# One core, gated cross-attention and quantised FFN: VectorE takes a slot's row maxima before the slot's other work

## The reference

```
x = x + tanh(g_xattn) * attention(layernorm(x), ctx)   # 16 heads of 16, rotary q and k, |i - j| <= 50, softmax, Wo
x = x + tanh(g_ffn)   * ffn(layernorm(x))              # 4-bit weights, 16-bit quantised activations, 256 -> 768 -> 256
```

## Time and profile before

| | us |
|---|---|
| median of 3 runs | 1548.13 (1544.25 to 1549.3) |
| the profiled execution's own time | 1547.24 |
| its span, first to last instruction | 1545.5 |
| TensorE busy in the span | 1308.7 (85%) |
| VectorE busy | 1264.0 (82%) |
| ScalarE busy | 827.3 (54%) |
| GpSimd busy | 675.6 (44%) |

### The profile page before, as it was taken

One profiled execution on the slowest core, in us unless ns is written; L12 is line 12 of the kernel. 1 busy time (PEld: TensorE's weight loads), 2 busy tenths in 40 slices (PEclk: granted clock), 3 DMA queues, 4 the chain that ended last, 5 costly groups with the idle time before them and its releaser, 6 DMA issues. The chain is left out here.

```text
span 1545.5 us, 31329 instructions
## 1 busy us (share of the span) xinstructions
PE 1308.7 (85%) x8992; PEld 847.5 (55%) x8992; DVE 1264.0 (82%) x3572; ACT 827.3 (54%) x1328; POOL 675.6 (44%) x1407
## 2 busy tenths in 40 slices
PE   2469999979898998979799876998999788874998
PEld 1446777656575665657567542443433333333887
DVE  5678998969787887969698734998999899995886
ACT  2225665646455463646456544665777466672332
POOL 0247777758676675757577640000000154541000
PEclk7679999999999998989899987999999989996999
DMA  3257566564736454546365411223454343434675
GB/s 103 70 118 161 131 149 153 137 148 99 168 97 146 113 132 110 137 109 146 97 160 141 101 35 41 102 102 130 175 195 174 122 163 129 157 132 136 228 231 176
DMA packets 132351, 206.89 MB, mean 134 GB/s; under 512 B 11160, under 2 KB 97051, under 8 KB 126107
## 3 DMA queue, kind: packets, MB, share of 16 engines
q1 hardware_dynamic: 132250, 205.86, 47.8%
HBM read 125.60 MB, written 79.69 MB: 133 GB/s over the span
## 5 line engine op out<-in xcount | busy, mean ns | idle before, releaser
L727 DVE CUSTOM_DVE_ANT_0 psum<-psum,band 128x178 f32<-128x178 f32 x1024 | 320.0, 372 | 62.8 <-PE psum L855 38.1
L607 ACT ACTIVATE probs<-psum 128x356 f32<-128x356 f32 x512 | 209.3, 461 | 295.5 <-PE psum L872 295.5
L1030 PE MATMUL psum<-xnT,w_upT 128*128 (+1 forms) x1152 | 269.7, 394 | 48.0 <-ACT u_int L1418 30.0
L538 POOL TENSOR_SCALAR_AFFINE_SELECT probs<-probs 128x154 f32<-128x154 f32 (+1 forms) x512 | 214.1, 427 | 218.5 <-ACT probs L607 213.6
L1030 PEld LDWEIGHTS psum<-xnT,w_upT 128*128 128x128 f16 x1152 | 113.4, 101 | 204.3 <-issue 77.2
L897 PE MATMUL psum<-probs,V 128*32 128x178 f32 x2048 | 206.9, 322 | 2.0 <-POOL probs L549 1.9
L855 PE MATMUL psum<-k_stack,q_stack 96*128 96x178 bf16 x1024 | 133.0, 247 | 70.9 <-DVE smax L727 57.0
L549 POOL TENSOR_SCALAR_AFFINE_SELECT probs<-probs 128x254 f32<-128x254 f32 (+1 forms) x512 | 189.1, 393 | 0.0
L1626 PE MATMUL psum<-w_downT,xnT 128*128 128x256 f16 x1152 | 128.0, 275 | 27.6 <-DVE xnT L1576 27.6
L727 DVE DVE_READ_ACCUMULATOR2_ANT smax<- 128x1 f32 x1024 | 143.8, 140 | 0.0
L855 PEld LDWEIGHTS psum<-k_stack,q_stack 96*128 96x128 bf16 x1024 | 80.1, 99 | 116.1 <-DVE smax L727 79.7
(11 more groups left out here) (189 smaller groups left out, 2382.4 us busy)
## 6 DMA issues: line engine op xcount, KB each, us to landing
k_parts_scratch<-k_parts SPq DMA_DIRECT2D x32, 384.0 KB, 2.6
q_parts_scratch<-q_parts SPq DMA_DIRECT2D x32, 384.0 KB, 2.6
k_stack<-k_parts_scratch SPq DMA_DIRECT2D x32, 384.0 KB, 5.2
q_stack<-q_parts_scratch SPq DMA_DIRECT2D x32, 384.0 KB, 5.0
gate_scratch<-g_stage SPq DMA_DIRECT2D x16, 768.0 KB, 3.3
g_in<-gate_scratch SPq DMA_DIRECT2D x16, 768.0 KB, 4.6
sig_scratch<-w_gateT SPq DMA_DIRECT2D x32, 384.0 KB, 2.3
sig_again<-sig_scratch SPq DMA_DIRECT2D x32, 384.0 KB, 3.5
```

Of the source, the lines that this page charges most:

```text
L538: nc.gpsimd.affine_select(out=t[:, :, 0:n], in_=t[:, :, 0:n], pattern=[[0, 2], [1, n]], compare_op=ALU.is_ge, fill=0.0, base=WINDOW - off, ...
L607: nc.scalar.activation(ring_tile(probs, b, pair, c)[:].rearrange("p e j -> p (e j)"), scoreT_bank[c][:, 0:2 * SPAN], ACT.Exp, scale=DK ** ...
L727: ins = nc.vector.tensor_tensor_reduce(out=mine, in0=mine, in1=keep["band"][:, t, :], scale=1.0, scalar=-3e38, op0=ALU.add, op1=ALU.max, a ...
L1030: last = nc.tensor.matmul(bank[:], weights[wp][:, c * I + f * P:c * I + (f + 1) * P], x_parts[:, c, bass.ds(j * (2 * TILE) + xp * TILE, TI ...
```

## The change

In each slot VectorE's `maxima` moves from behind six pieces of work to the head of the slot. The work itself, the semaphores, and every other engine's program stay as they are.

```diff
                 for slot in range(SLOTS):
+                    pair, late = pair_at(slot, S_FIRST)
+                    maxima(Batch(rnd, unit, late), pair)
                     if slot == 0:
                         residual(b4)
                     if slot == 1 and b0.fixed and 0 <= b0.n < NBUF:
...
                         remainder(b0, "q")
                     if slot == 7:
                         shift_parts(b1, 0)
-                    pair, late = pair_at(slot, S_FIRST)
-                    maxima(Batch(rnd, unit, late), pair)
                     if slot == 5:
                         divide(b3, 1)
```

## The result

The changed kernel takes 1723.12 us (median of 4 runs, 1719.57 to 1739.21) against 1548.72 (1544.25 to 1550.9): 1.115 times as long by the means, 95% interval 1.1076 to 1.1225. The prediction had the side right and the size wrong: 1645 us, range 1588 to 1692.

A forecast was written before the change was run, and what follows sets the result against it. TensorE was taken to bound the kernel (22.96 of 23.70 us a unit), VectorE close behind (21.82). Sum: 1547.24 + 112 (28 full units) + 7 (other units) - 21 (loop head) = 1645 us, range 1588 to 1692.

The forecast's parts named there:

- The waits: New TensorE waits in each unit: 3.94 us more, +112 us over 28 full units and +7 for the others.
- Slot 3: Shift rows come later, behind rope k, divide and the maxima, so TensorE waits: +2.2 us a unit.
- T6: Transposes of the second layernorm in slot 6 wait for ScalarE's late copy of V: +0.45 us a unit.
- ST of slot 6: Transposed scores of slot 6 wait for exponentials that ScalarE finishes late: +1.3 us a unit.
- K: The k projection waits for slot 0's residual, now behind the maxima: start at 2.95 in place of 2.75, +0.2 us.
- the 0.25 at slot 5: Transposed scores of slot 5 wait for ScalarE's exponentials, delayed by the k remainder: +0.25 us a unit.
- the gain in slot 4: Slot 4's scores no longer wait for the maxima of slot 3, now early: -0.46 us a unit.
- The ends: Units outside the 28 full ones: 3 us each for units 2 and 3, one for unit 32, +7 us.
- slot 3 alone is over: Against the faster rival (chance 0.04): slot 3's term by itself exceeds the 1.5 us a unit that rival allows.
- the rival that it falls: TensorE's clock falls after the new waits in each unit: +73 us, so 1718 us; chance 0.06.
- The loop: Six returns to the loop's head, 10.5 us each before, give back 3.5 us each: -21 us (0 to -30).
- the second case that I worked out: At a loop return, VectorE's second hold falls between maxima and residual: k projection 7 us late, 0 to 3.5 us back.

The follow-up runs named there:

- the slot 2 run: Maxima moved to the head of slot 2 alone, against the kernel before, loop kept: 1633.33 us.
- the filled runs: The changed order with overwritten matmuls put into TensorE's waits of slots 3 and 6: 1656.65 us with the loop, 1600.45 us with the loop written out.
- the filled kernel: The changed kernel, loop kept, with 28 overwritten matmuls ahead of slot 3's shift transposes and 22 ahead of slot 6's transposed scores: 1656.65 us.
- the version written out: The changed kernel with its three-unit loop written out on every engine, no matmuls added: 1616.32 us.

## Why the prediction was right and wrong

The spans of five versions split the 177.3 us: waits alone 122.6; clock in the looped kernel 59.4; and the loop, which costs 1545.5 - 1476.1 = 69.4 us with the old order and 1663.4 - 1598.7 = 64.7 with the new, so -4.7. That the parts add up is so by the way they are taken, and each rests on single executions: by medians, where there are several runs, they are 120.8, 66.5 and -11.8. The forecast had 119 (112 and 7), nothing, and -21.

*The waits* were right, by place, cause and size: 3.83 us in a unit (27.36 - 23.53) against 3.94 worked out. Slot 3 came at 2.0 for 2.2, T6 at 0.4 for 0.45, ST of slot 6 at 1.1 for 1.3, K at 0.16 for 0.2. Two terms were off and cancel: the 0.25 at slot 5 is not seen as a wait in unit 7, and the gain in slot 4 is smaller than the 0.46 forecast, as the unit before is 23.53 us outside the loop and not 23.70. The ends were mis-sized: 122.6 - 28 x 3.83 = 15 us for 7, nearly all in the units that fill the pipeline. One remark of the prediction was wrong: that "slot 3 alone is over" 1.5 us a unit. Its 2.2 us take in what moves in slot 2; by themselves slot 3 costs 1.31 us, slot 2 2.20 and slots 4 and 5 1.85, and these overlap. A small slip stands in the range: its own terms give 1645 + 22 + 21 = 1688, not 1692.

*The step that failed* is the clock: its term was put at nothing in the sum, and the rival that it falls at a chance of 0.06. It was what happened, and the prediction had named a unit's clock under 1.00 as a sign of being wrong. I dismissed it by one row, a wait of 3.75 us with the same four matmuls at 0.47 behind it, and that row was read too soon. The rows that follow it in the same trace of before:

```profile
878.49 0.70 PE L872 MATMUL psum<-q_stack,k_stack 98*128 98x178 bf16 x4
879.12 1.41 PE L897 MATMUL psum<-probs,V 128*32 128x178 f32 x8
...
883.80 0.80 PE L897 MATMUL psum<-probs,V 128*32 128x178 f32 x8
```

and the granted clock of one microsecond in it:

```profile
880.00:881.00 1.00, 1.00 (x8) 0.54 (x5) 0.02 (x1) 0.42 (x1) 0.87 (x3) 0.50 0.00 0
```

The clock did fall behind that wait, some 0.7 us after TensorE started again, and stayed at the lower level until about 882. It is the same picture as in the unit from 424.46, where it fell some 1.5 us behind the end of the slot 3 wait. So the row that was to speak against the rival spoke for it. What I had was also the price, 2.6 us a return (the slot 2 run later showed about 3 us a fall), and units whose TensorE had been busy 22.96 of 23.70 us and was now to stand some 4 us longer in each. What none of the rows shows is that waits of 2 us and less are enough, and that they are so in one unit and not in the next: unit 7 and the unit from 424.46 have the same slot 3 wait without and with the fall. That the rival's sum, 1718, lies 5 us from the result is in part luck: it has 73 us for the clock where 59.4 were measured, and -21 for the loop head where it was -4.7. The Trainium skill, page "TensorE: Matmul & The Clock Gate", Part 1, ties the clock to how busy the engine has been recently, and the filled runs agree with it: 28 and 22 idle-time matmuls a unit bring the clock back to 1.00 and 59.4 us with it.

*The loop* gave back 4.7 us by the spans (11.8 by medians), not 21. In the filled kernel a unit with a return takes 36.38 us on average, 8.5 over its neighbours, where it was 10.4 before: the six heads give back some 11 us. The loop's 21 units take 6 of them again, as away from the head they are 0.48 us longer than written out, where it was 0.18 with the old order. VectorE's timeline there, after:

```profile
489.51 0.35 DVE L727 CUSTOM_DVE_ANT_0 psum<-psum,band 128x178 f32<-128x178 f32 x1 [5.41 <-issue]
...
493.71 0.08 DVE L727 DVE_READ_ACCUMULATOR2_ANT smax<- 128x1 f32 x1 [2.95 <-issue]
493.95 0.75 DVE L769 SCALAR_TENSOR_TENSOR x<-psum,tanh,x 128x512 f32<-128x512 f32 x1 [0.16 <-issue]
```

The second hold falls within the maxima, ahead of their last accumulator read. That is the second case that I worked out, the one with 0 to 3.5 us back for each return, with the hold still a little earlier; the sum took 3.5. The residual starts 4.44 us behind M, K behind it, and TensorE runs slow after the return as before (3.75 us for K's eight matmuls at 494.85). That both holds stay, and the second after about as many instructions (7 in the profile, 5 before), is what the prediction took from the Trainium skill's page "Runtime: NRT & Kernel Launch", section "Instruction fetch mechanics"; the trace agrees, and with the loop written out both holds are gone. What it didn't get from there is where the second falls.

*What stays open*: what tells a unit in which the clock falls from one with the same waits in which it does not. The loop's returns and the filling of the pipeline come before many such units, but in the version written out a unit at 1.00 stands between two that are not, and in the changed kernel units 10 and 11 have the clock down before any return. Neither did I try to fill the waits at the loop head.

## What to carry to other kernels

An engine that is nearly as busy as the bottleneck must do its other work in the time it would wait for it; an order that puts the dependent work first turns that time into idle time on both. Follow the moved work to everyone who waits for it, here a second engine's in-order queue, before calling it covered. And when TensorE gets new waits in every unit of a long stretch, price the clock too, as a likely term and not as a remote one: here it was a third of the loss, and filling the waits with idle-time matmuls told it apart. Whether a wait lowered the clock is not seen in the first row behind it; read on for a few microseconds, or ask for the granted clock there.

## What the runs showed that I had not expected

Fifty useless matmuls in each unit made the kernel 66 us faster. Waits of 1.2 and 0.95 us in a unit brought the clock to 0.50 in some units and left it at 1.00 in others, and one wait of 1.57 us did the same. The first matmuls behind a wait of 3.75 us still ran at full clock (0.47 us for four); the fall to 0.50 came some 0.7 us later, and any look at that first row alone misses it. The jump back in the loop cost 69.4 us of span in six returns, the slightly longer units of the looped program (23.7 for 23.53 us) counted in, and writing the loop out (1479.65 us) took all of it away.
